# Two attention layers over 16 graphs: one unbroken run of 32 graphs in place of two layer programs

## What is computed

```python
h = relu(layernorm(x))
# layer 0
q, k, v = h@Wq0 + bq0, h@Wk0 + bk0, h@Wv0 + bv0           # split in 12 heads
s = q@k.T / sqrt(32) + beta * adj;  s = where(adj > 0, s, -9e15)
x = x + softmax(s) @ v
h = relu(layernorm(x))
# layer 1
q, k, v = h@Wq1.T, h@Wk1.T, h@Wv1.T + bv1
s = q@k.T / sqrt(384) + 2 * adj
p = where(any(s != 0), softmax(s), 0)                      # per row
x = x + (p @ v) @ Wo1.T + bo1
```

## Time and profile before

| | us |
|---|---|
| median of 3 runs (lowest, highest) | 2229.5 (2227.84, 2229.7) |
| the profiled execution | 2227.39 |
| its span, first to last instruction | 2225.6 |
| TensorE busy | 1990.9 (89%) |
| VectorE busy | 1865.0 (84%) |
| ScalarE busy | 1643.7 (74%) |
| POOL busy | 1072.6 (48%) |
| mean granted TensorE clock | 0.961 |

### The profile page before, as it was taken

One profiled execution on the slowest core, in us unless ns is written; L12 is line 12 of the kernel. 1 busy time (PEld: TensorE's weight loads), 2 busy tenths in 40 slices (PEclk: granted clock), 3 DMA queues, 4 the chain that ended last, 5 costly groups with the idle time before them and its releaser, 6 DMA issues.

```text
span 2225.6 us, 52690 instructions
## 1 busy us (share of the span) xinstructions
PE 1990.9 (89%) x19584; PEld 1285.9 (58%) x19584; DVE 1865.0 (84%) x4056; ACT 1643.7 (74%) x4151; POOL 1072.6 (48%) x1541
## 2 busy tenths in 40 slices
PE   2899999999999999994499999999999999999984
PEld 1565555656555555552366666666666666666652
DVE  1999999999999999992388888888898888898881
ACT  2898888888888888882387777777777777777761
POOL 5566565565665666521433444443453434443421
PEclk8899999999999999997699999999999999999997
DMA  4688999898988888886477898888898888988784
GB/s 97 131 203 205 211 228 219 215 220 208 216 211 211 213 217 204 207 193 149 111 179 168 185 210 186 186 181 198 186 208 187 181 194 186 208 190 188 164 184 97
DMA packets 114511, 419.28 MB, mean 188 GB/s; under 512 B 35408, under 2 KB 38480, under 8 KB 114256
## 3 DMA queue, kind: packets, MB, share of 16 engines
q1 hardware_dynamic: 77392, 306.81, 61.1%
q0 software_dynamic: 36864, 109.09, 20.6%
HBM read 88.61 MB, written 25.17 MB: 51 GB/s over the span
## 4 chain that ended last, share of the span: by engine, by line
PE 35%; DVE 7%; ACT 5%; DMA 2%; issue 1%; SPq 1%; POOL 1%; DVEq 0%; POOLq 0%
PE ring L258 9%; PE sc L236 7%; PE ring L282 6%; PE out L309 6%; DVE s L374 4%; PE ring L263 3%; ACT s L503 3%; DVE pt L388 2%; PE ring L249 2%; ACT pl L521 1%; PE ring L273 1%; SPq L210 1%; DMA pk<-pt 1%; DMA bob<-in_bo 1%; PE ring L268 1%
## 5 line engine op out<-in xcount | busy, mean ns | idle before, releaser
L503 ACT ACTIVATE s<-s,nmax 128x512 f32<-128x512 f32 x1536 | 1093.6, 724 | 265.7 <-DVE nmax L374 265.2
L374 DVE CUSTOM_DVE_ANT_0 s<-sc,bias 128x512 f32<-128x512 f32 x1536 | 968.5, 686 | 123.6 <-PE sc L236 77.4
L388 DVE STREAM_TRANSPOSE pt<-s 128x2048 f32<-128x2048 f32 x288 | 663.9, 2305 | 6.3 <-issue 6.1
L236 PE MATMUL sc<-k,q 32*128 32x512 f32 x3072 | 450.0, 655 | 81.5 <-DVE nmax L374 77.6
L659 POOL TENSOR_TENSOR v<-v,bvb 128x384 f32<-128x384 f32 x128 | 130.3, 1018 | 539.4 <-ACT v L541 539.0
L309 PE MATMUL out<-pk,v 128*32 128x192 f32 x6144 | 305.8, 342 | 55.2 <-DMA pk<-pt 55.0
L503 ACT ACTIVATION_READ_ACCUMULATOR s<-s,nmax 128x1 f32 x1536 | 308.7, 201 | 0.0
L309 PEld LDWEIGHTS out<-pk,v 128*32 128x32 f32 x6144 | 186.3, 113 | 207.6 <-issue 92.3
L236 PEld LDWEIGHTS sc<-k,q 32*128 32x128 f32 x3072 | 124.6, 187 | 197.7 <-DVE nmax L374 122.3
L258 PE MATMUL ring<-hT,wq 128*128 128x512 f32 x864 | 235.8, 418 | 3.0 <-DVE hT L400 3.0
L263 PE MATMUL ring<-wv,hT 128*128 128x384 f32 x1152 | 236.4, 350 | 0.0
(11 more groups left out here) (79 smaller groups left out, 2042.0 us busy)
## 6 DMA issues: line engine op xcount, KB each, us to landing
pk<-pt SPq DMA_DIRECT2D x1536, 192.0 KB, 6.0
bias<-in_adj POOLq DMA_DIRECT2D x128, 192.0 KB, 6.5
xin<-in_x POOLq DMA_DIRECT2D x64, 192.0 KB, 6.4
res<-in_x POOLq DMA_DIRECT2D x64, 192.0 KB, 9.3
x_between<-res POOLq DMA_DIRECT2D x64, 192.0 KB, 6.6
xin<-x_between POOLq DMA_DIRECT2D x64, 192.0 KB, 6.7
res<-x_between POOLq DMA_DIRECT2D x64, 192.0 KB, 5.5
out_x<-res POOLq DMA_DIRECT2D x64, 192.0 KB, 5.4
```

What stands on the lines that cost most here:

```text
L236: mm = nc.tensor.matmul(m.sc[:, j, :], m.q[rows, at, P * t:P * (t + 1)], by_number(k) if t < TURNS else k, start=True, stop=True)
L374: nc.vector.tensor_tensor_reduce(out=m.s[:, t % 2, :, j, :], in0=m.sc[:, j, :].rearrange("p (n e) -> p n e", e=P), in1=m.bias[par][:, t, : ...
L388: nc.vector.transpose(out=to, in_=m.s[:, t % 2].rearrange("p a j (i e) -> p (a j i) e", e=HD)).then_inc(turned, 1)
L503: nc.scalar.activation(tile, tile, ACT.Exp, bias=m.nmax[at][:, t, j:j + 1], scale=-1.0, accum_out=m.sums[at][:, t, j:j + 1]).then_inc(exp_ ...
```

## The change

The two programs become one, `two_layers`, over 32 graphs: graph g belongs to layer g // 16. Every engine walks all 32 x 3 x 4 steps in one loop, so that the items which prepare the next graph also run in graph 15 and prepare graph 16, layer 1's first. The ring's places are counted through all items, with no filler.

- **Opening.** SP loads x of graph 0 first, then beta, bq, bk, then the weights, then two bias rows. Each weight, x and the small loads have semaphores of their own. POOL's first loads are adj. VectorE waits for the small loads, then takes the statistics. Scores of step (0,t) wait for bias tile t alone. POOL makes bias tile 0 ahead of x's next load, and the first addition of v's bias comes between tiles 2 and 3.
- **Layer 1's weights.** They are loaded one by one into a room of 1280 columns that holds POOL's sums in layer 1. SP issues Wv's load behind the copies of (14, chunk 2); behind the copies of (15, chunk 0) it waits for Wv's split and issues Wq's, waits for Wq's split and issues Wk's, waits for v's biases and issues bo's. Wo's load is behind the copies of (16, chunk 1). ScalarE rounds them at the ends of steps (1,0), (1,2), (2,1) of graph 15, VectorE splits at the ends of (1,1), (1,3), (2,1).
- **Spread.** `keep` ends in a product of 4x4x32 = 512 columns, both operands broadcast over the 32 features, into `rwide`; spread is 4 transposes of 128x128.
- **sum_bias** runs over two tiles at a time, six additions in place of three.
- **Closing.** The remaining products of chunk 1 and the `pl` part of chunk 2 come ahead of the last spread on TensorE.

```diff
-def layer_program(nc, layer, x_in, adj, wq, wk, wv, wo, bq, bk, bv, bo, beta, x_out, mem):
+ROUNDINGS = {(B - 1, 1, 0): 2, (B - 1, 1, 2): 0, (B - 1, 2, 1): 1}
+SPLITS = {(B - 1, 1, 1): 2, (B - 1, 1, 3): 0, (B - 1, 2, 1): 1}
+def two_layers(nc, x, adj, weights, bq, bk, bv, bo, beta, x1, out, mem):
...
+            for a in range(QUADS):
+                sp.dma_start(m.xin[own(a)], tokens(x[0], a)).then_inc(x_first, 16)
+            sp.dma_start(m.beta[:], beta.rearrange("(a n) -> a n", a=1).to_broadcast([P, 1])).then_inc(small_in, 16)
+            sp.dma_start(m.bq[:], bq).then_inc(small_in, 16)
+            sp.dma_start(m.bk[:], bk).then_inc(small_in, 16)
+            for n in range(3):
+                load_weight(0, n)
+            load_row(m.bva, bv[0], bv_in[0])
+            load_row(m.bvx, bv[1], bv_in[1])
+            for g in range(GRAPHS):
                 for c in range(STEPS):
-                    move(part, b, c, par)
+                    move(g, c)
+                    if (g, c) == (B - 2, 2):
+                        load_weight(1, 2)
+                    if (g, c) == (B - 1, 0):
+                        for n, last in ((0, 2), (1, 0)):
+                            sp.wait_ge(weights_split[last], 2)
+                            load_weight(1, n)
+                        sp.wait_ge(v_added, NT * B)
+                        load_row(m.bva, bo, bo_in)
+                    if (g, c) == (B, 1):
+                        sp.wait_ge(res_added, NT * B)
+                        sp.dma_start(m.wo[:], weights[1][3].rearrange("(t p) n -> p t n", p=P)).then_inc(wo_in, 16)
...
                 if kind == "spread":
-                    pe.wait_ge(recip_done, DT * g + i + 1)
+                    pe.wait_ge(recip_done, nth("spread", g, i))
                     for t in range(NT):
-                        for j in range(HC):
-                            mm = nc.tensor.matmul(to[HD * j:HD * (j + 1), P * t:P * (t + 1)],
-                                                  m.recip[(par + d) % 2][:, t, HC * i + j:HC * i + j + 1].to_broadcast([P, HD]),
-                                                  m.ident[:], start=True, stop=True)
+                        mm = nc.tensor.transpose(to[:, P * t:P * (t + 1)], m.rwide[:, t, :], m.ident[:])
...
-            for kind, d, i in closing(layer):
-                if kind == "post" and i == 0:
-                    pv(B, -1, DT - 2, HALVES, B % 2, False)
-                    for n in range(PARTS):
-                        pv(B, -1, DT - 1, n, B % 2, False)
-                item("closing", kind, d, i, B, B % 2)
+            pv(GRAPHS - 1, DT - 2, HALVES)
+            pv(GRAPHS - 1, DT - 1, 0)
+            for x in CLOSING:
+                if x[0] == "post" and x[2] == 0:
+                    pv(GRAPHS - 1, DT - 1, 1)
+                    pv(GRAPHS - 1, DT - 1, 2)
+                item(*x)
...
+                if c == 0:
+                    if layer == 0:
+                        dve.wait_ge(bias_done, NT * b + t + 1)
...
+                for half in range(2):
+                    tiles = slice(2 * half, 2 * half + 2)
+                    n = 6 * b + 3 * half
+                    frm = m.bias[g % 2][:, tiles, :]
+                    nc.gpsimd.tensor_tensor(m.part[:], frm[:, :, 0:N // 2], frm[:, :, N // 2:N], ALU.add).then_inc(part_done, 1)
...
-                r = m.recip[par][:, :, HC * c:HC * (c + 1)]
-                nc.gpsimd.tensor_tensor(r, r, m.mz[:], ALU.mult).then_inc(recip_done, 1)
+                if n:
+                    pool.wait_ge(ready["spread"], n)
...
+                nc.gpsimd.tensor_tensor(m.rwide[:].rearrange("p t (j e) -> p t j e", e=HD), wide(m.recip[g % 2][:, :, HC * c:HC * (c + 1)]),
+                                        wide(m.mz[:]), ALU.mult).then_inc(recip_done, 1)
...
+            load_adj(0)
...
+            rstd(0)
+            pool.wait_ge(small_done, 2)
+            bias(0, 0)
             pool.wait_ge(ready["hT"], DT)
             load_x(1)
+            bias(0, 1)
+            bias(0, 2)
+            add_bv(0, 0)
+            bias(0, 3)
+            load_residual(0)
```

More of the change, by code:

```diff
@@ L72, in others @@
-    return out + more.get((c, t), [])
-def pv_in_step(c, t):
-    return {0: (*chunk_ahead(c, -2), 2), 1: (*chunk_ahead(c, -1), 0), 2: (*chunk_ahead(c, -1), 1), 3: None}[t]
-def opening():
-    return [("hT", 1, i) for i in range(DT)] + [("qk", 1, 0), ("qk", 1, 1), ("v", 1, 0), ("v", 1, 1)]
-def closing(layer):
-    out = [("spread", -1, DT - 1)] if layer else []
-    return out + [("post", -1, i) for i in range(NT)]
-def runs(part, d):
-    return not (part == "first" and d < 0 or part == "last" and d > 0)
@@ new lines, in in_step, with exists, step_before, pv_in_step @@
+    return [x for x in out + more.get((c, t), []) if exists(*x)]
+def exists(kind, g, i):
+    return 0 <= g < GRAPHS and (layer_of(g) == 1 or kind not in ("zero", "spread"))
+def step_before(g, c, t):
+    n = (DT * g + c) * NT + t - 1
+    return in_step(*chunk(n // NT), n % NT) if n >= 0 else []
+def pv_in_step(g, c, t):
+    if t == TURNS:
+        return None
+    s = DT * g + c - (2 if t == 0 else 1)
+    return (*chunk(s), (2, 0, 1)[t]) if s >= 0 else None
+OPENING = [("hT", 0, i) for i in range(DT)] + [("qk", 0, 0), ("qk", 0, 1), ("v", 0, 0), ("v", 0, 1)]
@@ new lines, with ring_places @@
+CLOSING = [("spread", GRAPHS - 1, DT - 1)] + [("post", GRAPHS - 1, i) for i in range(NT)]
+def ring_places():
+    steps = [x for g in range(GRAPHS) for c in range(STEPS) for t in range(NT) for x in in_step(g, c, t)]
+    slot, replaces, held = {}, {}, [None] * RING
+    for n, x in enumerate(OPENING + steps + CLOSING):
+        slot[x], replaces[x] = n % RING, held[n % RING]
+        held[n % RING] = x
+    return slot, replaces
+ROUNDINGS = {(B - 1, 1, 0): 2, (B - 1, 1, 2): 0, (B - 1, 2, 1): 1}
@@ new lines, in _ @@
+            dve.wait_ge(small_in, 48)
+            nc.vector.tensor_scalar(m.nbeta[:], m.beta[:], -1.0, None, ALU.mult).then_inc(small_done, 1)
+            nc.vector.tensor_scalar(m.bqs[:], m.bq[:], -scale[0], None, ALU.mult).then_inc(small_done, 1)
+            stats(0, range(NT))
+            aggregate(0)
+            for n in range(3):
+                split_low(0, n)
+            for x in OPENING:
+                if x[0] == "hT":
+                    item(*x)
+            for g, c, t in steps():
+                s = DT * g + c
+                scores(g, c, t)
+                if t == 1 and s >= 2 and layer_of(chunk(s - 2)[0]):
+                    scale_out(*chunk(s - 2))
+                if t == 0 and s:
+                    recip(*chunk(s - 1))
+                for x in step_before(g, c, t):
+                    item(*x)
+                if t:
+                    turn(g, c, t - 1)
+                if g + 1 < GRAPHS:
+                    if (c, t) == (0, 0):
+                        stats(g + 1, (0, 1))
+                    if (c, t) == (1, 0):
+                        stats(g + 1, (2, 3))
+                        aggregate(g + 1)
+                if (g, c, t) in SPLITS:
+                    split_low(1, SPLITS[g, c, t])
@@ L790, in _ @@
-            body("first", 0, 0)
-            for b in range(1, B - 1):
-                body("middle", b, b % 2, more=b < B - 2, again=b > 1)
-            body("last", B - 1, (B - 1) % 2)
-            residual(B - 1)
-            if layer:
-                add_bo(B - 1)
-                keep(B - 1, DT - 1, (B - 1) % 2)
-            else:
-                for i in range(NT):
-                    add_residual(B - 1, i)
-            store(B - 1)
-            pool.wait_ge(x_stored, LOADS * B)
+            bias(0, 1)
@@ L805 @@
+            load_residual(GRAPHS - 1)
+            add_bo(GRAPHS - 1)
+            keep(GRAPHS - 1, DT - 1)
+            store(GRAPHS - 1)
+            pool.wait_ge(x_stored, LOADS * GRAPHS)
 class Memory:
```

743 lines of the change are left out of this document (322 added, 421 removed).

## The result

The changed kernel took 2127.75 us (median of 4 runs, 2126.74 to 2130.22); the kernel before, on the same chip, 2228.67 us (median of 4, 2226.99 to 2229.7). The ratio is 0.955, with a 95% interval of 0.9533 to 0.9566. Forecast were 2118.7 us in a range of 2102 to 2134. So it is faster, inside the range and at the upper edge of the forecast's own ends (2109 and 2128), and 100.9 us were gained where the sum said 108.7. The spans of the two profiled executions, 2225.6 and 2125.2 us, differ by 100.4; from here on I compare those, stage by stage.

The account below looks back on a forecast made before the run. VectorE (94% busy) bounds layer 0 and TensorE (99%) layer 1, with time lost in opening, seam and tail. Gains 21.9 + 68.5 + 13 + 5.3 = 108.7 off 2227.4 give 2118.7 us, range 2102 to 2134.

Parts of the forecast that it names:

- The opening: Start to VectorE's first scores: 57.1 us falls to 35.2 with POOL's bias tiles hidden, gain 21.9.
- The seam: Drain, reload and restart between the layers: 138.4 us less an ordinary graph and added costs, gain 68.5.
- I take 4 for SP and DMA together, **8** in all: Cost of layer 1's weights in graph 15: 4.3 for splits and roundings plus 4, ends 2 and 16.
- rival 3: Seam jams on SP: late wq holds ScalarE, VectorE, SP, then TensorE at pk; 10 to 15 more, about 2131; chance 0.13.
- Graph 16: Layer 1's first graph costs 1.7 us more, as it carries graph 15's light post items, 12 transposes.
- The spread: Four transposes replace 32 passes on TensorE in layer 1: 0.52 less a chunk, counting in two of three; gain 13.
- The 0.2 for POOL: Per layer-1 graph, TensorE 1.0 earlier and POOL 0.5 later leave the slack behind q's copy short by 0.2 us.
- Rival 1: The spread's saving counts in all chunks of layer 1: 24 instead of 13, so 2108; chance 0.12.
- rival 2: The spread gives nothing: each transpose costs its length, or POOL's later rstd eats the gain; 2132, chance 0.15.
- keep's product: POOL's product in keep grows from 16 to 512 columns, 1.28 us by the nearest row, hidden: costs nothing.
- Rival 4: Slower than before, by a wait for keep in every chunk of layer 1; 2232 if its product takes 14.5; chance 0.01.
- The closing: The tail: products of chunk 1 run ahead of the last spread, SP's last eight copies land earlier; gain 5.3 us.

Follow-up runs that it names:

- all_bias: Changed kernel, but VectorE waits for all four bias tiles at a layer-0 graph's first scores, as before; first scores at 40.4 us, profiled span 2130.8 us.
- old_bias_order: Changed kernel with VectorE waiting for all four bias tiles and POOL making them behind its loads and v's addition; first scores at 52.0, span 2142.3 us.
- no_weights: Changed kernel without loading, rounding or splitting layer 1's Wq, Wk, Wv (layer 0's used, so numerically wrong); 2114.68 us, ratio 0.950.
- wv_early: Changed kernel with Wv's load issued two chunks earlier, behind the copies of (14, chunk 0); graph 15 68.1 us, profiled span 2115.0 us.
- pool_loads: wv_early with Wq's and Wk's loads issued from POOL's queue instead of SP's; 2118.89 us, ratio 0.952.
- old_closing: Changed kernel with the last spread again ahead of the products of chunk 1's second half; profiled span 2127.9 us.
- after_again: Changed kernel unaltered, timed again beside wv_early_store and seam2; 2122.49 us, ratio 0.9535.
- tile_store: Changed kernel with the last store issued tile by tile behind each output tile; profiled span 2133.1 us.
- wv_early_store: Changed kernel with Wv's load two chunks earlier and the last store tile by tile; 2120.36 us, ratio 0.9531.
- seam2: wv_early_store plus Wq and Wk loaded by POOL, Wv's and Wq's splits and Wk's rounding one step earlier; 2120.44 us, ratio 0.9522.

## Why the prediction was right, and where it was not

- **The opening** (21.9 taken, 23.0 measured): right, and so is its reason; all_bias and old_bias_order bring the wait for POOL back with the releaser named in the earlier trace rows. Two of its parts were off in opposite directions. wv was rounded from 17.34, not 16.3. And from transposes to scores it took 13.1, not the 15.15 of layer 1's old restart, which the step took over as if both openings ran alike. They didn't: in the old restart the granted clock was 0.5 (1.2 GHz) until 1092.0, and its first six products with wq took 2.90; in the changed kernel's opening it was 1.00 from 24.1 on, and the nine took 2.32.
- **The seam** (68.5 taken, 61.5 measured): here lies the error. The step that failed is "I take 4 for SP and DMA together, **8** in all". It measured 13.8 in graph 15 (73.9 against 60.1), of which 11.8 are the weights (no_weights). The upper end of that step, 16, "DMA in full, and splits", is not the sum that it names: 9.5 and 4.3 are 13.8; that this is what was measured is a coincidence, for the time did not go into bytes at full pace. The 4.3 for splits and roundings were small too, the split of wk with its wait costs 3.2 in step (2,1) instead of 2.2; but the great part, 5.5 in step (1,3), is wq's landing. I had costed DMA as bytes, partly free, and SP as issues. What decided was a queue in time: wv's bytes stood in front of the copies, the copies in front of wq (wv_early), and the rounding of wq, in ScalarE's order, in front of k's copy and of TensorE's scores (read from the rows). That is rival 3's mechanism at ScalarE, at 6 us more than taken instead of 10 to 15. Its first link, SP, does not bind once wv is early (pool_loads) and is untried in the changed kernel; its last, TensorE at pk, doesn't appear: in the trace TensorE stands for k. The argument against it, "the landings are two steps apart", counted on transfer engines with room, and these were 87% busy. The idle time comes back a second time, as a lower clock (0.88 against 0.97 in no_weights), in steps (1,3), (2,0) and (2,3). This part of the price is read from the rows; no run held the clock fixed.
- **Graph 16** (1.7 taken): 3.0 here, 1.5 in most other executions.
- **The spread** (13 taken, 12.1 measured with graph 31): right in mechanism, place and size. It counts in (2,3) to (0,0) and (0,3) to (1,0) and not behind (1,3). By steps, the layer-1 graph went from 4.7 to 4.2 in (0,0) and from 4.8 to 4.3 in (1,0), and nothing moved in (2,0). An undisturbed graph gained 1.02 to 1.04, which is 2 x 0.52. The 0.2 for POOL were right in one way: ScalarE's wait for nmr grew from 3.76 to 3.97 a graph, the sign named was above 4. They are not paid as a rule, since q's copy held TensorE up in only 2 of 13 graphs; the mean of 0.89 near my 0.84 is partly luck. Rival 1 is refuted by (2,0), rival 2 by the 0.49. With it falls, for this kernel, what the Trainium skill, "TensorE: Matmul & The Clock Gate", Part 4: PE-mode transpose, says of a transpose's length, if it is read as cost. The page's length agrees with the trace, 273 ns in the median of one (L271); but four of them last 0.66 together and hold the next item up for 0.49. The granted clock stayed at 1.00, 2.4 GHz, in the stretch with them.
- **keep's product** (nothing taken, 1.3 long by the nearest row): 1.05 and hidden. In the closing alone spread waits for it, 4.43, and the products behind it still wait 0.33 for pk. Rival 4 has nothing for it.
- **The closing** (5.3 taken, 2.7 measured): the order gives what was said, 4.6 between the traces up to the last products and 5.8 by old_closing. Behind it 1.8 are lost: from the last store's issue to the end it is 15.4 in the changed kernel and 15.3 in after_again and in old_closing, against 13.6 before, though the store lands in 3.3 in both. The trace puts 1.6 of it in POOL's DRAIN, 7.90 before and 9.54 in all variants but four: 7.91 in pool_loads, where POOL issues two loads more, 10.52 in tile_store and wv_early_store with their twelve additional stores, 8.89 in seam2 with both. So it moves with what POOL issues and not with the order of the closing; by what rule, no run shows, and it is left open. The sum had no term for it.

By the spans the total was off by 8.3 us, 5.8 of it one term that had been estimated by halves ("part is absorbed") though its ends, 2 and 16, lay far apart. That the sum is not further off is partly luck: the opening and graphs 0 to 14 gave 2.4 more than taken, of which 1.3 come from graphs that the change leaves alone.

## What to carry to other kernels

Start a prefetch when its place comes free, not when its consumer comes near: bytes that go out when the transfer engines have a backlog already push back every later transfer, and an engine that works in order passes the lateness on to what stands behind the waiting instruction. When a transfer is late, ask first what was queued in the transfer engines ahead of it, and only then who issued it. And when several edits are mixed with a total that scatters by 5 us, put the stages side by side, down to the step; one changed stage showed 5.8 us that the total hid.
